# Sorting four batches' rows by expert for the second feed-forward of a macaron block

## The reference

```
x = x + 0.5 * ffn(LN(x))
x = x + attention(LN(x))        # 16 heads of 64, one shared K and V head
x = x + 0.5 * ffn(LN(x))        # the same weights as the first

ffn(x):  logits = x @ gate_w + gate_b            # 8 experts
         probs  = softmax(logits) over the 512 tokens of a batch
         vals, idx = top_k(probs, 2)              # per token
         y[e] = relu(relu(relu(x@w1[e]+b1[e])@w2[e]+b2[e])@w3[e]+b3[e])   # 128x128 weights
         v[e] = sum over ALL tokens of y[e] * w_tok[:, e]    # w_tok is 0 where e is not chosen
         out[token] = sum of v[e] over the two chosen experts
```

## Time and profile before

| | us |
|---|---|
| median of three runs | 1052.49 |
| span of the profiled execution | 1048.3 |
| median of the runs less that span | 4.2 |
| TensorE, DVE, ACT, POOL busy in it | 1015.9, 763.9, 632.1, 700.0 |

### The profile page before, as it was taken

One profiled execution on the slowest core, in us unless ns is written; L12 is line 12 of the kernel. 1 busy time (PEld: TensorE's weight loads), 2 busy tenths in 40 slices (PEclk: granted clock), 3 DMA queues, 4 the chain that ended last, 5 costly groups with the idle time before them and its releaser, 6 DMA issues.

```text
span 1048.3 us, 18768 instructions
## 1 busy us (share of the span) xinstructions
PE 1015.9 (97%) x7176; PEld 661.9 (63%) x7176; DVE 763.9 (73%) x1027; ACT 632.1 (60%) x900; POOL 700.0 (67%) x369
## 2 busy tenths in 40 slices
PE   7999998899999999999999999999999999998996
PEld 6676886545657566556655665745565565776884
DVE  6879998877875676567576587546757636779996
ACT  4785556756754565456475477467746456775553
POOL 5555655766886588488488578756849757565653
PEclk9999999999999999999999999999999999999999
DMA  5721520000100100001001010001000103521612
GB/s 169 237 86 58 183 84 21 1 2 23 42 23 22 42 24 22 22 23 43 22 23 43 3 42 23 22 25 40 22 23 23 42 25 102 182 81 49 209 67 81
DMA packets 30253, 59.62 MB, mean 57 GB/s; under 512 B 10437, under 2 KB 15702, under 8 KB 30166
## 3 DMA queue, kind: packets, MB, share of 16 engines
q1 hardware_dynamic: 30096, 58.41, 18.4%
q10 hardware_dynamic: 70, 0.02, 0.0%
HBM read 55.27 MB, written 2.62 MB: 55 GB/s over the span
## 4 chain that ended last, share of the span: by engine, by line
PE 83%; DVE 10%; ACT 2%; issue 2%; POOL 2%; DMA 0%; DVEq 0%; ACTq 0%; POOLq 0%
PE ring L1038 20%; PE ring L972 6%; PE ring L1050 6%; PE ring L996 5%; PE ring L1002 5%; PE ring L998 5%; PE ring L1000 5%; PE ring L742 4%; PE ring L748 4%; PE ring L744 4%; PE ring L1011 3%; PE ring L766 2%; PE ring L765 2%; PE ring L768 2%; DVE ring L1576 2%
## 5 line engine op out<-in xcount | busy, mean ns | idle before, releaser
L1728 DVE TENSOR_REDUCE mx<-ring 128x2 f32<-128x1024 f32 x248 | 290.3, 1226 | 64.1 <-PE ring L972 64.1
L627 POOL TENSOR_TENSOR sum_picksT<-sum_picksT,P_wb 128x1024 f32<-128x1024 f32 x128 | 310.7, 2427 | 18.9 <-POOL sum_picksT L627 0.9
L1356 ACT ACTIVATE P_wb<-ring 128x1024 f32<-128x1024 f32 x256 | 262.1, 1026 | 54.2 <-PE ring L1002 24.6
L627 POOL TENSOR_TENSOR sum_picksT<-P_wb 128x1024 f32<-128x1024 f32 x64 | 167.0, 2610 | 167.8 <-ACT P_wb L1356 167.8
L686 POOL TENSOR_TENSOR R<-t,R 128x512 fp32r<-128x512 f32 x124 | 162.1, 1308 | 124.5 <-ACT R L1166 121.2
L1038 PE MATMUL ring<-P_wb,t 128*32 128x512 f32 x2048 | 228.4, 593 | 0.0
L1038 PEld LDWEIGHTS ring<-P_wb,t 128*32 128x32 f32 x2048 | 74.0, 110 | 138.6 <-issue 120.0
L1368 ACT COPY OZ<-ring 128x512 f32<-128x512 f32 x64 | 37.4, 585 | 157.3 <-PE ring L1038 148.6
L1166 ACT CAST R<-t 128x512 fp32r<-128x512 f32 x124 | 76.9, 620 | 74.6 <-PE ring L748 68.2
L972 PE MATMUL ring<-R 64*128 64x512 f32 x512 | 104.8, 407 | 1.0 <-ACT P_wb L1344 0.7
L996 PE MATMUL ring<-R 64*128 64x512 f32 x512 | 102.0, 393 | 1.5 <-DVE MR L1733 1.5
(11 more groups left out here) (199 smaller groups left out, 1529.9 us busy)
## 6 DMA issues: line engine op xcount, KB each, us to landing
P_wb<-wd SPq DMA_DIRECT2D x64, 512.0 KB, 4.8
rzb<-rzd SPq DMA_DIRECT2D x64, 256.0 KB, 3.9
xs<-in_L_attn_x SPq DMA_DIRECT2D x8, 256.0 KB, 5.2
zrc<-SZ SPq DMA_DIRECT2D x128, 2.0 KB, 1.7
out<-xs SPq DMA_DIRECT2D x8, 256.0 KB, 2.7
sum_picksT<-in_L_ffn_w SPq DMA_DIRECT2D x2, 512.0 KB, 5.6
MR<-mT SPq DMA_DIRECT2D x62, 4.0 KB
t<-in_L_ffn_w SPq DMA_DIRECT2D x1, 512.0 KB, 7.3
```

Source lines behind the costliest of these rows:

```text
L627: pool.tensor_tensor(US[:, g % 2, c, :, :], first, PU[:, TPB * c + t, :, :], ALU.add).then_inc(s_ua, 1)
L1356: act.activation(PU[:, u, :, :], ring[slot(("scores", g, u))][:, :, :], ACT.Exp, scale=SCALE).then_inc(s_exp, 1)
L1728: dve.tensor_reduce(mx[:, :, u] if g else mx0_unit[:, u // TPB, :, 0, u % TPB, 0], ring[slot(("max", g, u))][:, :, :], AX.X, ALU.max).then ...
```

## The change

Only the second feed-forward's batches 0 to 3 are computed in another way. All 16 dense units on them go. In their place:

- During the attention, after an earlier top-2 (groups 21 to 24), VectorE computes for each of the 2048 tokens and its two choices the row number in a list sorted by expert, each expert's part rounded up to whole tiles of 512 rows (place_rows, in group 25). With 4096 rows and 8 experts that is at most 15 tiles. ScalarE builds rows of 128 normalized features and 8 weights (fill_rows), and GpSimd sends them to the DRAM list with 32 indirect DMAs of 128 rows (send_rows: six each in groups 25 to 29, two in group 30). The list (15 x 512 rows of 544 bytes) is zeroed during the first feed-forward by five DMAs from SP.
- The second feed-forward has 24 units: 8 routed ones with two tiles each (the last with one), then the 16 dense ones on batches 4 to 7.
- A routed unit loads its two tiles (557 KB, load_sorted), TensorE turns them (gather, 8 transposes), ScalarE takes the high part (sorted_high), and VectorE picks each row's weight and makes the low part (sorted_low). SP writes those weights to DRAM, waits for the write, and loads them broadcast (spread_row_weights).
- The tile's expert is known only at run time, so GpSimd reads its number into a register and copies that expert's weights of all three layers, 128x768 elements, for each tile (copy_weights). Biases are chosen per tile; split1 and reduce3 of a routed unit therefore run half by half.
- TAIL is packed into the first eight units; the top-2 of batches 4 to 7 ends after the last routed unit, and the dense units' token weights are sent and loaded then. The token weights of batches 0 to 3 are sent no more.
- wex replaces whi and wlo (the same numbers, laid out expert by expert); some semaphores are merged.

The first two pieces are the order of the work, the next two are on SP, copy_weights is on GpSimd and sorted_low on VectorE.

```
         def unit_steps(f):
             if f:
-                steps = [("layer1", 0), ("split", 0), ("sums", NQ - 1), ("normal", 2), ("layer1", 1), ("split", 1), ("layer2", 0)]
+                steps = [("copy", 1), ("layer1", 0), ("split", 0), ("sums", NQ - 1), ("gather", 1), ("layer1", 1), ("split", 1),
+                         ("reciprocals", NQ - 1), ("gather", 2), ("layer2", 0), ("copy", 2)]
             else:
                 steps = []
-            for u in range(NU):
-                if u + 2 < NU:
+            for u in range(UNITS_OF[f]):
+                if routed(f, u + 3):
+                    steps.append(("gather", u + 3))
+                if u + 2 < UNITS_OF[f]:
                     steps += [("layer1", u + 2), ("split", u + 2)]
...
+        TAIL = {0: [("copy", 3), ("scale", NQ - 1), ("normal", 4)],
+                1: [("copy", 4), ("out", B - 1), ("turn", 4), ("normal", 5)],
+                2: [("copy", 5), ("moments", 8), ("root", 8), ("turn", 5), ("logits", 4), ("normal", 6)],
+                3: [("copy", 6), ("invert", 8), ("turn", 6), ("logits", 5), ("normal", 7)],
+                4: [("copy", 7), ("turn", 7), ("logits", 6)],
+                5: [("logits", 7), ("largest", 1), ("exp", 1)],
+                6: [("invert_sum", 1), ("probs", 1), ("turn_probs", 1), ("choose", 0)],
+                7: [("choose", 1), ("choose", 2), ("choose", 3), ("picks", 1)]}
...
+            def load_sorted(u):
+                if u == 0:
+                    for k in range(2):
+                        sp.wait_ge(s_sent[k], 16 * sent_before(len(FILLS) + k))
+                    sp.wait_ge(s_st, UNITS * (NQ - 2))
+                elif u <= 2:
+                    sp.wait_ge(s_sf, NQ - 2 + u)
+                if u >= 2:
+                    sp.wait_ge(s_rx, u - 1)
+                    sp.wait_ge(s_rw, u - 1)
+                n = len(halves_of(1, u))
+                rows = xg[2 * TS * u:2 * TS * u + TS * n, :].rearrange("(k p j) c -> p k (j c)", p=P, j=BLOCKS)
+                sp.dma_start(sorted_of(u)[:, 0:n, :, :].rearrange("p k j c -> p k (j c)"), rows).then_inc(s_sorted[u % 2], 16)
+            def spread_row_weights(u):
+                n = len(halves_of(1, u))
+                sp.wait_ge(s_rw, u + 1)
+                sp.dma_start(wg[u, 0:n].rearrange("k p j -> p k j"), row_weights[u % 2][:, 0:n, :]).then_inc(s_rwd, 16)
+                sp.wait_ge(s_rwd, 16 * (u + 1))
...
+                else:
+                    sp.wait_ge(F[1]["l3_drained"], u - RING + 1)
+                sp.dma_start(PU[:, u % RING, 0:n, :], wg[u, 0:n].rearrange("k p j -> k (p j)").partition_broadcast(P)).then_inc(s_wb[u % RING], 16)
             def late_weights():
...
+                spread_sums(NQ - 1)
+                load_sorted(1)
+                spread_row_weights(0)
                 send_reciprocals(NQ - 1)
+                for u in range(2, RU):
+                    load_sorted(u)
+                    spread_row_weights(u - 1)
+                spread_row_weights(RU - 1)
+                send_weights(1, 1, GW[1][1]["wT"])
...
+            def copy_weights(u):
...
+                elif u == 1:
+                    pool.wait_ge(s_pv, UNITS * NQ)
+                    pool.wait_ge(s_ua, (TPB - 1) * PAIRS * NQ)
+                elif u >= 4:
+                    pool.wait_ge(F[1]["l3_done"], u - 3)
+                for k in halves_of(1, u):
+                    e = pool.value_load(expert_int[0:1, 2 * u + k:2 * u + k + 1], min_val=0, max_val=E - 1)
+                    ins = pool.tensor_copy(tile_weights(u, k).rearrange("p l h o -> p (l h o)"),
+                                           wex[:, bass.ds(e, 1), :, :, :].rearrange("p e l h o -> p (e l h o)"))
+                ins.then_inc(s_tw, 1)
+            def sorted_low(u, pair):
...
+                tiles = of_expert[:, 2 * u:2 * u + n, :].unsqueeze(2).to_broadcast([P, n, BLOCKS, E])
+                choice_link(dve.tensor_tensor(row_products[:, 0:n, :, :], sorted_of(u)[:, 0:n, :, P:ROW], tiles, ALU.mult))
+                dve.tensor_reduce(row_weights[k][:, 0:n, :], row_products[:, 0:n, :, :], AX.X, ALU.add).then_inc(s_rw, 1)
+                high, low = x_of(1, u)
+                dve.wait_ge(s_rxh, u + 1)
+                dve.tensor_tensor(low[:, 0:n, :], pair[:, 0:n, :], high[:, 0:n, :].bitcast(F32), ALU.subtract).then_inc(s_rxl, 1)
```

More of the change, by code:

```diff
@@ L44, in macaron_kernel @@
     SCALE = float(DK) ** -0.5
+    TS = 4 * P
+    BLOCKS = TS // P
+    RT = 2 * TPB * TPB * P // TS + E - 1
+    RU = (RT + 1) // 2
+    MISSING = 2 * RU - RT
+    UNITS_OF = (NU, RU + NU // 2)
+    LAST = (UNITS_OF[0] - 1, UNITS_OF[1] - 1)
+    ROW = P + E
+    FILL = 3
+    FILLS = [range(t, min(t + FILL, TPB * TPB)) for t in range(0, TPB * TPB, FILL)]
     assert D == P and E == 8 and DK == 64 and TPB == 4 and HPQ == 4
@@ new lines, in macaron_kernel @@
+        before = tables[:, 0:P]
+        ring_rows = tables[:, P:P + 2 * FILL * ROW].rearrange("p (t c) -> p t c", c=ROW)
+        up_to = [tables[:, P + 192 * k:P + 192 * (k + 1)] for k in range(2)]
+        products = tables[:, 4 * P:6 * P].rearrange("p (k t e) -> p k t e", k=2, e=E)
+        row_of_all = tables[:, 6 * P:7 * P].rearrange("p (t e) -> p t e", e=E)
+        LEFT = P + 2 * FILL * ROW
+        count_up = tables[:, LEFT:LEFT + 2 * E]
+        running = [tables[:, LEFT + 2 * E + 12 * k:LEFT + 2 * E + 12 * (k + 1)] for k in range(4)]
@@ L160, in xnT, with h2_of, routed, halves_of @@
         def xnT(f, b):
-            return PT[:, b % TPB, :] if f else OT[:, b, :]
+            return (lg0[:, :], US_flat[:, 13 * 2 * P:13 * 2 * P + S])[b % 2] if f else OT[:, b, :]
         h1h, h1l = ([R[:, 2 * E + 2 * k:2 * E + 2 * k + 2, :], MR[:, k, :, :]] for k in range(2))
-        h2h, h2l = (R[:, 2 * E + 2 * k:2 * E + 2 * k + 2, :] for k in range(2, 4))
-        def h2_of(u):
-            return (h1h[0], h1l[0]) if u == NU - 1 else (h2h, h2l)
+        h2h, h2l = R[:, 2 * E + 4:2 * E + 6, :], H2L
+        def h2_of(f, u):
+            return (h1h[0], h1l[0]) if u == LAST[f] else (h2h, h2l)
+        def routed(f, u):
+            return f == 1 and u < RU
+        def halves_of(f, u):
+            return range(min(2, RT - 2 * u)) if routed(f, u) else range(2)
+        def halves_done(f, u, k=None):
+            last = len(halves_of(f, u)) - 1 if k is None else k
+            return 2 * u + last + 1 - (MISSING if f and u >= RU else 0)
+        def lows_done(f, u, k):
+            return u + 1 - (MISSING if f and k and u >= RU - 1 else 0)
+        def dense(f, u):
+            d = u - RU if f else u
+            return (TPB // 2 if f else 0) + d // E, d % E
+        def nth(f, b):
+            return b + 1 - (TPB if f else 0)
+        def x_of(f, u):
+            start = 2 * (u % 2) if routed(f, u) else 2 * dense(f, u)[0]
+            return xh[:, start:start + 2, :], xl[:, start:start + 2, :]
+        def tile_weights(u, k):
+            return WTR[:, u % 4 - 1, k, :, :, :] if u % 4 else WT0[:, k, :, :, :]
+        def weights_of(f, u, k, layer, part):
+            if routed(f, u):
+                return tile_weights(u, k)[:, layer, part, :]
+            return wex[:, dense(f, u)[1], layer, part, :]
+        def bias_of(f, u, k, layer):
+            if routed(f, u):
+                return tile_bias[:, layer, 2 * u + k:2 * u + k + 1]
+            e = dense(f, u)[1]
+            return (nb1, bcol[:, R_B2:R_B2 + E], nb3)[layer][:, e:e + 1]
+        def low_by_dve(f, u, k):
+            return k == 1 and u >= LAST[f] - 1
+        def weight_loads(f, slot, before_dense=True):
+            return B // 2 * f + (len(range(slot, RU, RING)) if f and before_dense and slot < RING else 0)
         assert UNITS == E and PAIRS == 2
@@ L692, in units @@
                         split2(f, arg)
+                    elif stage == "copy":
+                        copy_weights(arg)
                     elif stage == "turn":
@@ L1610, in choose_first, with clear_places @@
                 dve.tensor_tensor(by_expert(wtk[:, 0, :, :]), by_batch(ind[:, 0:n, :]), by_column(pt), ALU.mult).then_inc(s["wtk_ready"], 1)
+            def clear_places():
+                dve.wait_ge(s_et, TPB)
+                for i in range(2 * E):
+                    dve.memset(count_up[:, i:i + 1], float(i))
+                for buffer in running:
+                    dve.memset(buffer[:, 0:TPB], 0.0)
+                for k in range(2):
+                    ins = dve.memset(up_to[k][:, 0:64], 0.0)
+                choice_link(ins)
```

605 lines of the change are left out of this document (391 added, 214 removed).

## The result

The changed kernel takes 1106.04 us (median of four, 1102.5 to 1109.0), the one before on the same chip 1052.3: the ratio is 1.051, 95% interval 1.047 to 1.055. It is slower by 54 us, as forecast in its sign, and 24 us above the forecast of 1082, at the very end of the range of 1061 to 1106. The profiled execution took 1102.5 us, its span is 1100.4, 52.1 more than that of before.

A forecast was written before the change was run, and what follows sets the result against it. TensorE was taken to bound the kernel, with the new chains keeping it from gaining; 22.1 to the first dense reduction, -1.6 catch-up, +4 clock and +5 attention gave +29.5, span 1077.8, median 1082, range 1061 to 1106.

The forecast's parts named there:

- what VectorE was to catch up behind it: First dense units after the boundary: VectorE regains 0.27 us in each of six units, -1.6 us.
- What bounds the kernel: Whole kernel: TensorE, busy 1015.9 of 1048.3 us; the rewritten second feed-forward stage is bound by TensorE's order.
- The rival by TensorE's count: Second feed-forward: units run at TensorE's matmul and transpose rate, 30 us gained, 1022; chance 0.06.
- Start, +33.0: Attention's end to first routed reduction: rows of units 1 and 2 load late behind SP's waits; 920.8 against 887.78.
- The two holes: Start: TensorE left idle from 882.5 to 890.2 and from 895.1 to 907.2.
- Clock, +4: Start: after each idle stretch transposes and a layer cost double at 1.2 GHz; 4 us, bounds 0 and 10.
- Price of a copy, 1.6 a tile: GpSimd's weight copies: 1.25 us plus 0.35 for the register per tile, 3.2 a unit.
- Routed units, -17.7: First to last routed start: 66.0 us against 83.7, GpSimd's copies behind its subtractions making 10.6 us a turn.
- Boundary, +6.8: Last routed to first dense reduction: late choice and sending of token weights uncovered, 11.0 us against 4.2.
- Attention, +5: Attention: indirect DMAs at 1.2 us delay GpSimd, 3 to 4 us reaching TensorE; VectorE's small operations cost 1.5.
- some 30 operations of 0.1 to 0.3: Attention, groups 24, 25 and 29: VectorE's counting and placing, with 22 tiny memsets, costs 1.5 us.
- The text's own test: Attention: the forecast counts as wrong if the attention is longer by over 15 us.
- The rival of 1107 (dear DMAs): Attention: indirect DMAs at 2.4 us each make it lose 30 us instead of 5, 1107; chance 0.13.

The follow-up runs named there:

- sp_early: Changed kernel with only SP's order altered: unit 1's rows loaded ahead of the last sums, unit 2's ahead of the last reciprocals; 1095.0 us.
- loads_copies: Changed kernel with weight copies issued earlier and SP's loads queued in the order in which they can start; 1090.5 us.
- v3_flat: v3 with the rows' weights laid out block by block, so the routed reduction reads without a stride and the write goes 4 bytes at a time; 1111.3 us.
- loads_gather: loads_copies with the turning of unit u+4's rows put ahead of the extra work of step u; 1085.8 us.
- v3: loads_gather with places, tables of tiles and unit 0's weight copy moved later in the attention, and the picks put later; 1080.9 us.

## Why the prediction was right in sign and 24 us short

The 24 us are the attention +16.1, the routed units +2.7, the boundary +2.1, what VectorE was to catch up behind it +1.2, start and clock together -1.4, the stretch ahead of the mark +1.9, and 1.4 by which the median lies further above the profiled span than before (5.6 us, 4.2 before).

- **What bounds the kernel.** Right. A stage bound by TensorE's order gained nothing from 153 fewer matmuls, since the new chains never let it run at that rate. The rival by TensorE's count fell with the first hole.
- **Start, +33.0.** Measured +35.6. The two holes came where they were put, 7.2 and 12.9 us long where 7.7 and 12.1 were forecast, and for the named reason: sp_early and loads_copies took 16 us off by SP's order alone.
- **Clock, +4.** Right in kind, and contained in the stages above: transposes at 1.94 instead of 1.09 us and layer 1 of unit 1 at 2.9 us where that of unit 0 took 1.7. Start and clock together were forecast at 37 and measured 35.6. Two places were not foreseen: the three layers behind the hole in the first turn, and the boundary, below. (The six matmuls of the earlier trace rows overlap the window's ends; they start 0.43 us apart, which is what "twice" rests on.)
- **Price of a copy, 1.6 a tile.** Twice what it measured: two copies take 1.6 us, 0.80 each, without a gap for the register. Of the pair at 949.47 the first takes 1.82, beside VectorE's product, and the second 0.82. The estimate from the Trainium skill (GPSIMD Engine Reference, Elementwise side-by-side cycle accounting), 1.15, was nearer and also too high.
- **Routed units, -17.7.** Measured -15.0. The first four turns took 47.6 us where 48.0 were forecast, but for a reason that was half wrong. With copies at 1.6 us the link was GpSimd's order in the first two turns only; in the others it was largely ScalarE's order, a cast behind work that waits, which I did not follow. The last three took 21.2 and not 18 (6.3, 5.7 and 9.2), and that is the last one: the first transposes of the probabilities wait for ScalarE, which waits for a reciprocal on VectorE that stands behind unit 6's reduction. This chain of the late softmax was put at nothing. Half a reduction also takes 1.15 us and not the 0.76 of the earlier trace rows, as its weights are read with a stride, but that is not the cause: in v3_flat, with 0.75, the same three turns take 5.1, 5.7 and 9.0.

```profile
1009.04 1.09 PE L1075 MATMUL ring<-ident,OZ 128*128 128x128 f32 x4 [4.30 <-ACT OZ L1409]
```

- **Boundary, +6.8.** Measured +8.9, by the chain that was named: no matmul from 1014.6 to 1020.5, while VectorE makes the second choice. But the clock was not hidden behind the load, as the prediction had it: it is granted at 0.66 from 1021 to 1028, the load has landed at 1027.44, and the first dense reduction starts at 1028.19, released by TensorE's layer 3. VectorE then had nothing to catch up, -0.4 and not -1.6.

```profile
1020.51 0.45 PE L1039 MATMUL ring<-ident,wtk 128*128 128x128 f32 x1 [5.94 <-DVE wtk L1976]
```

- **Attention, +5: the step that failed.** It measured +21.1, which is 16 of the 24 us. The DMAs were priced well (1.26 us against 1.2) and cost 7.0 us where 3 to 4 were allowed. The 1.5 us for "some 30 operations of 0.1 to 0.3" is the term that was mis-sized: the places and the tables cost 12.0. Another 2.1, for the earlier gate, the choice and the filling of the rows, stood in no term. I had the row that says so, twelve elements in 2.16 us beside an addition; I used it for the routed units, where GpSimd is often idle, and not for the attention, where it is nearly always adding and where every such wait stands ahead of the row maxima. The text's own test, an attention longer by over 15 us, came out against it.
- **The rival of 1107 (dear DMAs)** has the measured time, but not its cause: at 2.4 us each the DMAs would have had to cost 30 us; they cost 7. That the time still lies in the range is in part luck: its upper part stood there for dear DMAs, and the chains on VectorE filled it.

## What to carry to other kernels

Price a small VectorE operation by what runs on GpSimd beside it and by what is queued behind it, not by its elements: two chains of 23 operations, most of 8 to 128 elements, cost 12 us here, and nine of the 23 waited for GpSimd. When work is moved into a stage that looks idle, write down each in-order queue around it, the DMA issuer's too; moving loads, copies and casts within three queues took 28 us off start and routed loop with not one instruction fewer (44.1 and 68.7 us in the changed kernel, 28.0 and 56.7 in loads_gather). And fewer matmuls are worth nothing while the chain that feeds them is longer than they are.

## What was not expected of the hardware

- Elementwise float32 operations on VectorE with one on-chip operand and a scalar, over 8 or 16 elements, can wait for GpSimd's additions as those with two operands do (9.79 us for eight over 16 elements, of which four waited). Reductions did not (0.72 for eight beside an addition), nor did the same form over one element (1.06 for eight).
- An operand read with a stride of four elements makes half a reduction 1.13 to 1.19 us instead of 0.75.
- A write of 4 KB in pieces of 4 bytes lands after 13.0 us, in pieces of 16 bytes after 3.9.
- Behind two waits of the same length before the same 64 matmuls the granted clock differed: 0.61 over the next 8 us in v3 (2.82 us of waiting), 1.00 in loads_gather (2.83).
- A GpSimd copy of 128x768 takes 0.80 us; an indirect DMA of 128 rows of 544 bytes holds the engine for 0.96 us, 1.26 from one to the next.
